# A GRU scan on one core: TensorE's loop body cut from four time steps to one pair of steps, with one PSUM bank per gate

## What is computed

```python
Xz = einsum('btc,hc->tbh', X, Wxz) + bxz          # the same for r and h
def step(H, xs):
    xz, xr, xh = xs
    Z = sigmoid(xz + H @ Whz.T + bhz)
    R = sigmoid(xr + H @ Whr.T + bhr)
    H_tilda = tanh(xh + R * H @ Whh.T + bhh)
    H_new = Z * H + (1.0 - Z) * H_tilda
    return (H_new, H_new @ Whq.T + bhq)
x = x + transpose(Ys)
```

## Time and profile before

| | |
|---|---|
| median of 3 runs | 2276.43 us (2246.28 to 2291.57) |
| the profiled execution | 2232.23 us |
| its span | 2230.3 us |
| granted TensorE clock, mean | 0.998 |
| PE busy | 2132.6 us (96%) |
| weight loads busy | 2054.4 us (92%) |
| DVE busy | 1589.5 us (71%) |
| ACT busy | 1226.0 us (55%) |
| POOL busy | 888.9 us (40%) |

### The profile page before, as it was taken

The page is one execution under the profiler, slowest core; times in us unless marked ns, Lnnn a source line. Parts: engine busy times, 40 slices in busy tenths (PEclk is TensorE's granted clock), DMA queues, the critical chain, the costliest instruction groups (busy, mean ns, idle before and its releaser), DMA issues.

```text
span 2230.3 us, 206497 instructions
## 1 busy us (share of the span) xinstructions
PE 2132.6 (96%) x88464; PEld 2054.4 (92%) x88464; DVE 1589.5 (71%) x9106; ACT 1226.0 (55%) x5994; POOL 888.9 (40%) x1830
## 2 busy tenths in 40 slices
PE   8899999999999999999999999999999999999997
PEld 7799999999999999999999999999999999999997
DVE  4777777777777777777777777777777777777776
ACT  2455555555555555555555555555555555555554
POOL 3344344444344443444443444434444434444331
PEclk9999999999999999999999999999999999999999
DMA  3000000000000100000000000000000000000000
GB/s 153 16 28 17 26 24 21 26 24 21 26 24 19 28 17 26 24 21 26 24 21 26 23 19 28 16 26 24 21 26 24 21 26 24 19 28 16 26 20 22
DMA packets 84278, 58.27 MB, mean 26 GB/s; under 512 B 9490, under 2 KB 75410, under 8 KB 83474
## 3 DMA queue, kind: packets, MB, share of 16 engines
q1 hardware_dynamic: 84240, 57.81, 8.7%
q10 hardware_dynamic: 4, 0.02, 0.0%
HBM read 41.01 MB, written 16.78 MB: 26 GB/s over the span
## 4 chain that ended last, share of the span: by engine, by line
PE 95%; issue 4%; DMA 1%; DVE 1%; ACT 0%; SPq 0%; DVEq 0%
PE u_bank L620 42%; PE v_bank L620 20%; PE y_bank L555 9%; PE d_bank L523 7%; PE b_bank L523 6%; PE a_bank L523 6%; PE c_bank L523 3%; DMA w_all<-in_w_x 0%; PE b_bank L540 0%; PE a_bank L540 0%; PE u_bank L540 0%; DVE pre_t L980 0%; PE c_bank L540 0%; DMA y_io<-in_x_res 0%; DVE scanned L1082 0%
## 5 line engine op out<-in xcount | busy, mean ns | idle before, releaser
L980 DVE STREAM_TRANSPOSE pre_t<-u_bank 128x32 f32<-128x32 f32 (+1 forms) x3072 | 455.1, 199 | 278.2 <-PE u_bank L620 241.4
L620 PE MATMUL u_bank<-wh,scanned 128*16 128x128 f32 (+1 forms) x16384 | 548.5, 273 | 82.8 <-issue 74.9
L317 POOL TENSOR_TENSOR x_parts<-z_of 128x96 f32<-128x96 f32 x744 | 341.6, 459 | 556.7 <-DVE h_sums L1000 243.1
L620 PE MATMUL u_bank<-wh,reset_state 128*16 128x128 f32 (+1 forms) x16384 | 556.4, 273 | 3.7 <-DVE reset_state L1133 2.5
L620 PE MATMUL v_bank<-wh,scanned 128*16 128x128 f32 (+1 forms) x16384 | 548.1, 273 | 0.0
L620 PEld LDWEIGHTS u_bank<-wh,scanned 128*16 128x16 f32 (+1 forms) x16384 | 428.5, 103 | 112.4 <-issue 103.7
L620 PEld LDWEIGHTS v_bank<-wh,scanned 128*16 128x16 f32 (+1 forms) x16384 | 460.9, 104 | 0.3 <-issue 0.2
L620 PEld LDWEIGHTS u_bank<-wh,reset_state 128*16 128x16 f32 (+1 forms) x16384 | 428.4, 103 | 18.2 <-DVE reset_state L1133 14.0
L968 ACT ACTIVATE scan_on<-pre_t 128x16 f32<-128x16 f32 (+1 forms) x1536 | 237.8, 219 | 288.8 <-DVE pre_t L980 288.8
L942 ACT ACTIVATE r_gate<-pre_t 128x16 f32<-128x16 f32 (+1 forms) x1536 | 234.5, 215 | 255.4 <-DVE pre_t L980 247.9
L317 POOL TENSOR_TENSOR z_of<-z_of 128x96 f32<-128x96 f32 x558 | 255.9, 459 | 275.5 <-DVE reset_state L1133 173.1
(11 more groups left out here) (141 smaller groups left out, 2848.9 us busy)
## 6 DMA issues: line engine op xcount, KB each, us to landing
y_io<-in_x_res SPq DMA_DIRECT2D x256, 64.0 KB, 2.0
out<-y_io SPq DMA_DIRECT2D x256, 64.0 KB, 1.6
x_all<-in_x_t SPq DMA_DIRECT2D x62, 256.0 KB, 2.6
w_all<-in_w_x SPq DMA_DIRECT2D x2, 1536.0 KB, 7.6
wh<-in_w_hr SPq DMA_DIRECT2D x1, 1024.0 KB, 10.7
wh<-in_w_hz SPq DMA_DIRECT2D x1, 1024.0 KB, 14.2
wh<-in_w_hh SPq DMA_DIRECT2D x1, 1024.0 KB, 16.2
wq<-in_w_q SPq DMA_DIRECT2D x1, 1024.0 KB, 6.4
```

The source lines that it names most:

```text
L317: nc.gpsimd.tensor_tensor(*of, ALU.add).then_inc(made, 1)
L620: mm = nc.tensor.matmul(gate_rows(g, par, slice(Q * j, Q * j + rows)), of, wh[g][:, m, P * j:P * (j + 1)], start=False, stop=(m == G - 1), ...
L980: nc.vector.transpose(flat(pre_t[g][:, a:b]), gate_part(g, par, a, b)).then_inc(done, 1)
```

## The change

- PE's loop body is one pair of steps. A third nested loop, over `odd`, picks the half of the half-turn: `If(odd)` with an `Else` stands between Z and H and behind H of both steps, so four times in a body, and holds what depends on it. `batch_gap` with its `If(later)` is inside the branches behind H. The `If_lt` are gone: the loop ends one turn sooner, and the last three half-turns are written out. The description of the change gives the loop as six blocks of instructions.
- No loop has `hint_back_edge`.
- R, Z and H have one bank each, the same for all pairs, and `scanned` has one place for a pair's two states.
- ACT puts the x part by three copies of 128 columns: R and Z in the second step of the pair before, H at the start of the pair (`put`). Two more copies in a half-turn, `keep_b` at c = 0 and `keep_a` at c = 2, save states that output products read later. The new state waits for these copies at c = 0 and c = 2 (last lines of the diff).
- Some waits of PE move to ACT (x_loaded, s_ready), and waits for weight sums (w_sub_made, w_sub3_made) stand a few products later.

```diff
-        scanned = sb("scanned", [P, 2, G, 3 * B, 2])
-        states = scanned[:, :, :, :, 1]
+        scanned = sb("scanned", [P, G, 3 * B, 2])
+        states = scanned[:, :, :, 1]
+        kept_a = sb("kept_a", [P, G, Q])
+        kept_b = sb("kept_b", [P, half, Q])
...
-        u_bank = [bank("u_bank0"), bank("u_bank1")]
-        v_bank = bank("v_bank")
+        gate_bank = [bank("r_bank"), bank("z_bank"), bank("h_bank")]
...
-        def state_before(c):
-            par, s = divmod(c, 2)
-            return states[:, 1 - par, :, 2 * B:3 * B] if s == 0 else states[:, par, :, B:2 * B]
+        def state_before(s):
+            return states[:, :, 2 * B:3 * B] if s == 0 else states[:, :, B:2 * B]
...
-            def recur(g, t, c):
-                par, s = divmod(c, 2)
+            def recur(g, t, s):
                 if isinstance(t, int) and t == 0:
                     pe.wait_ge(wh_loaded[g], 16)
                 for m in range(G):
@@ -614,135 +607,183 @@
                     if g == H:
                         of = reset_state[:, m, B:2 * B] if s == 0 else reset_state[:, m, :]
                     else:
-                        of = state_before(c)[:, m] if s == 0 else states[:, par, m, 0:2 * B]
+                        of = states[:, m, 2 * B:3 * B] if s == 0 else states[:, m, 0:2 * B]
                     rows = B if s == 0 else 2 * B
                     for j in range(G):
-                        mm = nc.tensor.matmul(gate_rows(g, par, slice(Q * j, Q * j + rows)), of,
+                        mm = nc.tensor.matmul(gate_bank[g][Q * j:Q * j + rows, 0:P], of,
                                               wh[g][:, m, P * j:P * (j + 1)], start=False,
                                               stop=(m == G - 1), skip_group_check=True)
                 mm.then_inc(pre_done[g], 1)
 
-            def half_turn(i, t, x_gap, first=False, end=False):
-                for c in range(4):
-                    par, s = divmod(c, 2)
-                    if s == 0 and not (first and par == 0):
-                        if first:
-                            pass
-                        else:
-                            pe.wait_ge(u_put[par], i)
-                    recur(R, t + c, c)
-                    if first and c == 0:
-                        plain_to(2, a_bank)
-                    if s == 0 and not first:
-                        pe.wait_ge(v_put[par], i)
-                    recur(Z, t + c, c)
-                    if first and c == 0:
-                        plain_to(3, b_bank)
-                    if c == 0:
-                        pe.wait_ge(ys2_ready, i + 1)
-                        q6()
-                    elif c == 1:
-                        pe.wait_ge(q16_copied, i + 1)
-                        q7()
-                    elif c == 2:
-                        if end:
-                            pe.wait_ge(yv_b_put, i)
-                        else:
-                            pe.wait_ge(q_filled, i + 1)
-                        q4()
-                    elif not end:
-                        pe.wait_ge(yv_a_put, i + 1)
-                        q2()
-                    recur(H, t + c, c)
-                    x_gap(c)
-                    if c == 1:
+            def pair(q, between, gap):
+
+
+                begin = isinstance(q, int) and q == 0
+                for s in range(2):
+                    t = 2 * q + s
+                    if s == 0 and not begin:
+                        pe.wait_ge(gate_put[R], q)
+                    recur(R, t, s)
+                    if begin and s == 0:
+                        plain_to(2, b_bank)
+                    if s == 0 and not begin:
+                        pe.wait_ge(gate_put[Z], q)
+                    recur(Z, t, s)
+                    if begin and s == 0:
+                        plain_to(3, c_bank)
+                    between(s)
+                    if s == 0 and not begin:
+                        pe.wait_ge(gate_put[H], q)
+                    recur(H, t, s)
+                    gap(s)
+
+            def outputs_between(c, i, first=False, end=False):
+
+                if c == 0:
+                    pe.wait_ge(ys2_ready, i + 1)
+                    q6()
+                elif c == 1:
+                    pe.wait_ge(q16_copied, i + 1)
+                    q7()
+                elif c == 2:
+                    pe.wait_ge(kept_b_ready, i + 1)
+                    if end:
+                        pe.wait_ge(yv_b_put, i)
+                    else:
+                        pe.wait_ge(q_filled, i + 1)
+                    q4()
+                elif not end:
+                    pe.wait_ge(yv_a_put, i + 1)
+                    q2()
+
+            def outputs_gap(c, i, first=False, end=False):
+
+                if c == 1:
+                    if first:
                         pe.wait_ge(yt_ready[0], 2)
-                        q5()
-                    elif c == 2:
-                        pe.wait_ge(ys4_ready, i + 1)
+                    q5()
+                elif c == 2:
+                    pe.wait_ge(ys4_ready, i + 1)
+                    if first:
                         pe.wait_ge(wq_loaded, 16)
-                        q3()
-                        if not end:
-                            q1()
-                    elif c == 3 and end:
-                        pe.wait_ge(y_filled, 2)
-                        project_y(0).then_inc(y_projected, 1)
+                    q3()
+                    if not end:
+                        pe.wait_ge(kept_a_ready, i + 1)
+                        q1()
+                elif c == 3 and end:
+                    pe.wait_ge(y_filled, 2)
+                    pe.wait_ge(kept_a_ready, i + 1)
+                    project_y(0).then_inc(y_projected, 1)
...
+            def batch_gap(c, k, later):
                 with pe.If(later):
-                    with pe.If_lt(pe.to_reg(n), turns - 2):
-                        batch_goes_on(c, n)
+                    batch_goes_on(c, k)
                 with pe.Else():
                     if c == 0:
-                        with pe.If(n):
-                            batch_ends(n)
-                    with pe.If_lt(pe.to_reg(n), turns - 2):
-                        batch_begins(c, n)
+                        with pe.If(k - 1):
+                            batch_ends(k - 1)
+                    batch_begins(c, k)
+
+            def last_gap(c):
+                if c == 0:
+                    batch_ends(turns - 2)
+
+            def pair_of_loop(k, later, odd):
+                i = 2 * k - 1 + later
+
+                def between(s):
+                    with pe.If(odd):
+                        outputs_between(2 + s, i)
+                    with pe.Else():
+                        outputs_between(s, i)
+
+                def gap(s):
+                    with pe.If(odd):
+                        batch_gap(2 + s, k, later)
+                        outputs_gap(2 + s, i)
+                    with pe.Else():
+                        batch_gap(s, k, later)
+                        outputs_gap(s, i)
+
+                pair(4 * k - 2 + 2 * later + odd, between, gap)
...
-            half_turn(0, 0, plain_gap, first=True)
-            with nc.Fori(0, turns - 1, engines=[mybir.EngineType.PE], head_slot={mybir.EngineType.PE: 0}, hint_back_edge=True) as n:
-                with nc.Fori(0, 2, engines=[mybir.EngineType.PE], hint_back_edge=True) as later:
-                    half_turn(2 * n + 1 + later, 8 * n + 4 + 4 * later, lambda c: batch_gap(c, n, later))
-            half_turn(2 * turns - 1, 8 * turns - 4, lambda c: None, end=True)
+            half_turn(0, plain_gap, first=True)
+            with nc.Fori(1, turns - 1, engines=[PE], head_slot={PE: 0}) as k:
+                with pe.Fori(0, 2) as later:
+                    with pe.Fori(0, 2) as odd:
+                        pair_of_loop(k, later, odd)
+            half_turn(2 * turns - 3, last_gap)
+            half_turn(2 * turns - 2, lambda c: None)
+            half_turn(2 * turns - 1, lambda c: None, end=True)
...
-            def put_u(par, values):
-                nc.scalar.copy(u_bank[par][:, 0:RH], values[:, 0:RH]).then_inc(u_put[par], 1)
-
-            def put_v(par, values):
-                nc.scalar.copy(v_bank[:, P * par:P * (par + 1)], values[:, RH:COLS]).then_inc(v_put[par], 1)
+            def put(g, values):
+                nc.scalar.copy(gate_bank[g][:, 0:P], values[:, X_AT[g]:X_AT[g] + P]).then_inc(gate_put[g], 1)
+
+            def keep_a(i):
+
+                if not isinstance(i, int) or i > 0:
+                    act.wait_ge(ys4_ready, i + 1)
+                    act.wait_ge(q2_done, i)
+                for h in range(N):
+                    act.wait_ge(state_ready[h], 4 * i + 3)
+                nc.scalar.copy(kept_a[:], states[:, :, B:3 * B]).then_inc(kept_a_ready, 1)
+
+            def keep_b(i):
+                if not isinstance(i, int) or i > 0:
+                    act.wait_ge(q34_done, i)
```

(75 more changed lines are left out.)

142 lines of the change are left out of this document (71 added, 71 removed).

## The result

| | time, us | runs |
|---|---|---|
| before | 2284.0 median (2246.28 to 2338.37) | 4 |
| changed | 2317.98 median (2315.94 to 2319.22) | 4 |

Ratio 1.025, 95% interval 1.013 to 1.037: slower, and clear of no change, though not surely by more than 2%. The ratio compares the four runs with the two fast ones of before (2246.28 and 2276.43 us), while the medians of all runs are 34 us apart, 1.5%. Against the profiled executions (2232.2 and 2317.0 us) the step is 84.8 us. The runs of the changed kernel lie within 3.3 us of each other and of their profile; those of before spread over 92 us, all above theirs.

A forecast was written before the change was run, and what follows sets the result against it. PE, 96% busy, bounds the kernel, its gaps mostly its own control. 2.30 us more a turn over 62 turns (143 us) and 3 us outside take the profiled 2232.2 to 2376; 22 us of excess gives 2398, range 2320 to 2450.

The forecast's parts named there:

- Stops in the loop: PE's halts for its own control, with 0.15 us for ACT: 3.93 us a turn against 1.63, 2.30 more.
- ends of `odd` = 0 pairs: PE's stop at the loop end after an `odd` = 0 pair, behind q5: 0.54 us, with `later` = 1 0.61.
- end of `later` = 0: PE's stop after the `odd` = 1 pair with `later` = 0: control 1.42 less cover 0.42, 1.00 us.
- of the outer body: PE's stop after the `odd` = 1 pair with `later` = 1: control 1.75 less cover 0.42, 1.33 us.
- gap at c = 0: Behind H at c = 0, `later` = 0: control 0.90 less cover 0.60, a stop of 0.30 us.
- head of the body: Instructions starting each loop body: two FUSED_REGOPS 0.36 us together, plus 0.10 for a third loop variable.
- the cover after a jump with q5 behind it: PE work queued at the `odd` = 0, `later` = 1 end: 0.23 us, since the jump before q5 eats cover.
- ACT's copies: `keep_a` at c = 2 delays the Z sigmoids and the new state: 0 to 0.5 us a turn, taken as 0.15.
- The excess of the runs over the profile: Runs lay 14 to 59 us over the profiled execution, median 44, cause unknown; half, 22 us, was carried.
- The rival that the body is fetched again in some executions: The large body is refetched in unprofiled executions, the small one not: 44 us off, 2376 us; chance 0.05.
- The rival of cheap taken branches: Taken branches stall PE no longer than untaken ones, 0.14 us each: 2.2 us a turn, 2289 us; chance 0.11.
- Without the hints taken branches fetch: Unhinted taken branches wait for fetches, 2.1 us at four ends a turn: 520 us, about 2890; chance 0.03.

The follow-up runs named there:

- `banks_alone`: The changed kernel with the old two PE loops and their hints, keeping the changed banks, puts and kept copies: 2217.9 us, ratio 0.989 to before.
- a near relative: The kernel before with its loops ending a turn sooner, the last three half-turns written out and both `If_lt` kept: 2254.1 us (2228.9 to 2340.5).
- `whole_turn`: The changed kernel with one loop whose body is a whole turn (2795 instructions, `later` written out, one hint): a turn grew to 41.8 us.
- padded kernel: The changed kernel with 96 products added in a never-taken branch inside the loop (1821 instructions instead of 1436): 4930.6 us.

## Why the prediction came out as it did

The direction and the mechanism were right: more time because of PE's own control, with work and waits for others unchanged. The time was 80 us too high: 2318.0 us lies 2 us below the range of 2320 to 2450. As a ratio to the 2276 us on record the range is 1.019 to 1.076, and the measured 1.025 is within it, near its lower end. Between the profiled executions the step is 84.8 us where 144 were forecast. The terms:

- **Stops in the loop**: 2.30 us more a turn forecast, 1.42 measured on average; 55 of the 80 us. By part, forecast and measured: ends of `odd` = 0 pairs 0.54 and 0.34, 0.61 and 0.34; end of `later` = 0 1.00 and 0.87; of the outer body 1.33 and 1.27; gap at c = 0 0.30 and 0.14. The prices of branches held (208 against 216 to 228 ns). Mis-sized was the head of the body: 0.46 with "0.10 for the third loop variable", 0.32 measured, four times a turn, 0.56 us. The other error is the cover after a jump with q5 behind it: I let the jump eat it (0.23), measured is the same 0.33 as without a jump. Handing over 16 pairs seems to cost next to nothing, which no run tests by itself.
- **A stop I put at nothing**: R at c = 3 loses 0.12 us twice a turn, where a jump and a count follow two 64-column products.
- **ACT's copies**: 0.15 us a turn forecast, none measured (`banks_alone`); the copies overlap by about 0.1 us, so one more in a row of them costs less than its 0.32 us.
- **The excess of the runs over the profile**: I carried half of the median's, 22 us, with no cause for it; the changed kernel has none (median 1 us over its profile). The rival that the body is fetched again in some executions has support: a burst of fetches, seen in a near relative. That length alone is the cause is out by three steady kernels with bodies over seven blocks.
- **Outside the loop**: 1 us forecast, about -3 measured (84.8 less 88 for the 62 turns). PE's first Z product begins at 22.5 us instead of 25.2, and the end is the same within 0.3; why the start is earlier stays open.

The rival of cheap taken branches is not out by the stops alone: their sum with the gap, 2.96 us, lies midway between its 2.2 and my 3.78, and the two short ones (0.34) are nearer to its 0.30 and 0.26. What rules it out is the sequencer: a taken compare holds it for 0.27 us, far over the 0.15 from which the rival would decide. *Without the hints taken branches fetch* is out for this kernel by q8: 27 blocks, and 27 with hints. Of the signs, "issue" was to grow to about 180 us in some 250 waits and grew to 118 in 126: the view leaves out the 124 stops of 0.14 us, 17 us together. The short stops were to show 0.34 and 0.41 and showed 0.14 each. PE's busy time was to stay at 2130 us and is 2163.7; the longer first gates that the forecast itself counts are part of it. The longer stops, the gates of 1.07 us, the wait for the scan and q8 came as said.

The change thus removed an excess too: against the median the loop's 100 us are half hidden, because an ordinary run of the kernel before takes some 50 us more than its profile. With the old loops the changed kernel is 0.989 of before, and with the closing branch moved 0.976; both ratios hold some of that excess.

## What to carry to other kernels

On an engine that is busy to 95%, a hardware loop's control is a cost like any other: list the sequencer's instructions between two products, add 0.065 us to each one's duration, and subtract what is queued ahead (by these traces some 20 pairs: 0.3 us of 64-column, 0.4 of 96-column, 0.6 of 128-column products). Put a closing branch behind the widest products and keep it apart from other jumps; that gained 37 us here, where a shorter body lost 100 and a longer one 490. When the runs of a kernel spread and its profiles don't, take the branches out one kind at a time, and shorten the body apart from that, before reading anything into a median.

## What was unexpected of the hardware

- A body of 1821 instructions with a never-taken branch over 384 of them fetched 1136 blocks, 4.9 ms, nine at a time; one of 1810 without it fetched none in the loop.
- In `whole_turn` each of the 11 blocks that a turn fetches costs about 0.7 us although PE works some 3 us on each, and a fetch takes 1.1 us (median). In the padded kernel a fetched block costs 2.4 us (78 us a turn, 18 blocks).
- `If_lt` in a body of 7.15 blocks spread the runs over 112 us, and in one of 6.96 over 12.
- The granted clock of the padded kernel was 0.77 on average over its two levels (1.2 and 2.4 GHz), and 0.82 with hints; its PE was busy 62% and stood still at most 5.9 us at a time in the loop. `whole_turn`, busy 83%, kept 0.999.
